# Layer-0 attention on one core: from ten slots to five phases in TensorE's order of work

## What is computed

```python
h, hd = 16, 64
q, k, v = ((x @ w).reshape(4, 1024, h, hd) for w in (w_q, w_k, w_v))
dot = einsum('bqhd,bkhd->bhqk', q / 8, k / 8)
dot = where(causal, dot, -inf)
att = softmax(dot, axis=-1)
out = einsum('bhqk,bkhd->bqhd', att, v).reshape(4, 1024, h * hd) @ w_u + b_u
```

## Time and profile before

| | us |
|---|---|
| median of 3 runs | 2423.7 |
| lowest and highest | 2411.78 and 2423.76 |
| span of the profiled execution | 2408.9 |
| TensorE busy in it | 2199.0 (91%) |
| VectorE busy | 1443.0 (60%) |
| ScalarE busy | 1224.4 (51%) |
| GpSimd busy | 1048.7 (44%) |

### The profile page before, as it was taken

The page is one execution under the profiler, slowest core; times in us unless marked ns, Lnnn a source line. Parts: engine busy times, 40 slices in busy tenths (PEclk is TensorE's granted clock), DMA queues, the critical chain, the costliest instruction groups (busy, mean ns, idle before and its releaser), DMA issues. The chain is left out here.

```text
span 2408.9 us, 40334 instructions
## 1 busy us (share of the span) xinstructions
PE 2199.0 (91%) x15428; PEld 1390.3 (58%) x15428; DVE 1443.0 (60%) x3248; ACT 1224.4 (51%) x1788; POOL 1048.7 (44%) x980
## 2 busy tenths in 40 slices
PE   4999999999999999994999999969999998897787
PEld 2555565555555565543888888724434455555667
DVE  3677757776677757773556565555554555656533
ACT  2555545554465545541323333267786876664533
POOL 0777757776677757773223232433333321100001
PEclk9999999999999999997999999979999999999999
DMA  2000000000000000001200000000000000003001
GB/s 76 1 1 1 1 1 1 1 1 1 1 1 1 1 1 1 1 1 35 39 1 1 1 1 1 1 1 1 1 1 1 1 1 1 2 8 71 1 1 36
DMA packets 36323, 18.19 MB, mean 8 GB/s; under 512 B 16666, under 2 KB 33956, under 8 KB 36132
## 3 DMA queue, kind: packets, MB, share of 16 engines
q1 hardware_dynamic: 36132, 15.61, 2.6%
HBM read 13.50 MB, written 2.10 MB: 6 GB/s over the span
## 5 line engine op out<-in xcount | busy, mean ns | idle before, releaser
L311 POOL TENSOR_TENSOR a_first<-a_first,a_ring 128x512 f32<-128x512 f32 (+3 forms) x352 | 558.8, 1588 | 141.9 <-ACT a_ring L556 106.5
L1764 ACT ACTIVATE g_probsT<-g_s_ps 128x1024 f32<-128x1024 f32 (+2 forms) x448 | 368.9, 868 | 136.6 <-PE g_s_ps L1633 83.3
L556 ACT ACTIVATE a_ring<-a_st 128x768 f32<-128x768 f32 (+1 forms) x256 | 234.6, 916 | 262.8 <-PE a_st L463 262.8
L478 PE MATMUL a_o_ps<-a_ring,a_v 128*64 128x512 f32 (+3 forms) x1280 | 249.2, 485 | 3.4 <-POOL a_ring L293 2.4
L645 DVE RECIPROCAL a_row_inv<-a_row_inv 128x512 f32<-128x512 f32 x64 | 213.8, 3342 | 16.8 <-ACT a_row_inv L544 16.8
L1034 ACT ACTIVATE m_silu<-m_up,m_b 128x512 f32<-128x512 f32 x160 | 109.6, 688 | 221.9 <-PE m_up L966 219.1
L623 DVE TENSOR_REDUCE a_part_max<-a_mx 128x2 f32<-128x1024 f32 x128 | 156.5, 1222 | 102.4 <-PE a_mx L434 99.1
L1664 PE MATMUL g_o_ps<-g_probsT,g_values 128*32 128x512 f32 (+5 forms) x2688 | 206.7, 419 | 5.5 <-POOL g_probsT L1509 5.1
L1633 PE MATMUL g_s_ps<-g_qT,g_kT 64*128 64x512 f32 (+3 forms) x896 | 172.7, 433 | 28.0 <-ACT g_probsT L1764 22.4
L1509 POOL TENSOR_SCALAR_AFFINE_SELECT g_probsT<-g_probsT 128x512 f32<-128x512 f32 x128 | 88.0, 691 | 246.1 <-ACT g_probsT L1764 246.0
L630 DVE CUSTOM_DVE_ANT_0 a_masked<-a_mx,mask_wide,a_part_max 128x256 bf16<-128x256 f32 (+3 forms) x256 | 128.3, 548 | 91.1 <-PE a_mx L434 90.6
(11 more groups left out here) (310 smaller groups left out, 4372.8 us busy)
## 6 DMA issues: line engine op xcount, KB each, us to landing
m_w<-in_L_ffn_rw SPq DMA_DIRECT2D x2, 1024.0 KB, 8.3
s_w<-in_L_ffn_w SPq DMA_DIRECT2D x1, 2048.0 KB, 9.0
s_w<-in_L_ffn_w SPq DMA_DIRECT2D x4, 512.0 KB, 10.2
out_x<-x SPq DMA_DIRECT2D x8, 256.0 KB, 2.3
m_w<-in_L_ffn_rw SPq DMA_DIRECT2D x2, 512.0 KB, 5.1
x<-in_L_attn_x SPq DMA_DIRECT2D x1, 512.0 KB, 4.5
a_outT<-in_L_attn_w_q SPq DMA_DIRECT2D x1, 512.0 KB, 5.4
a_outT<-in_L_attn_w_k SPq DMA_DIRECT2D x1, 512.0 KB, 6.0
```

The lines of the kernel that those rows point to most:

```text
L311: pool.tensor_tensor(total[:, h, q:q + w], total[:, h, q:q + w], probs_of(n, u)[:, h, off:off + w], ALU.add).then_inc(added, 1)
L478: last = pe.matmul(o_ps[rows_of(h), first_q:first_q + w], v_half[n // 4 % 2][:, j, head:head + A_HD], probs_of(n, u)[:, h, off:off + w], s ...
L556: act.activation(probs_of(n, u)[:, :, 0:w], st_ps[u % 2][:, :, 0:w], ACT.Exp).then_inc(exp_done, 1)
L1764: act.activation(out, src.rearrange("p k (j n) -> p k j n", j=at_once), ACT.Exp, scale=float(HD) ** -0.5).then_inc(exp_done, 1)
```

## The change

The ten slots of a pair become five phases t = 0 to 4. In each, TensorE scores units 2t and 2t + 1 and computes the phase's maxima ahead of them, between them and behind them (`MAXES_FIRST`, `MAXES_MIDDLE`, `MAXES_LAST`); then it transposes inputs, does `output` where there is one, weighs units 2t - 2 and 2t - 1 and does `add_rows`; then it does the side work. No instruction of the scores, maxima, values or projections is added or taken away. `output` is split into two column halves of 64, so that it has the form of `weigh`. The value block of phase 1 goes through `mx_ps[:, 0]` instead of `p_ps`. `add_rows(n, 0)` comes in phase 2. The projection k = 0 of a pair moves to the pair before (phase 4) and the order of keys and queries in the second half is exchanged. The loops of ScalarE and VectorE follow the phases; GpSimd's does not change.

```diff
-MAXES_EARLY = {0: (0, 7), 3: (1, 0), 6: (1, 3), 7: (1, 4), 8: (1, 5), 9: (1, 6)}
-MAXES_LATE = {0: (0, 8), 1: (0, 9), 3: (1, 1), 4: (1, 2)}
-PROJECTIONS = {0: 0, 1: 1, 3: 2, 4: 3}
-INVERSES = {2: 0, 5: 1}
-FINISHING = {1: {6: (0, 1), 7: (1, 2), 8: (2, 4), 9: (4, 5)}, 2: {8: (5, 6), 9: (6, 7)}}
-NORMALIZING = {2: {6: (0, 2), 7: (2, 4)}, 3: {2: (4, 5)}}
-BLOCKS_FINISHED, BLOCKS_NORMALIZED = {6: 0, 7: 4}, {6: 0, 8: 4}
+MAXES_FIRST = {0: (0, 7), 2: (1, 1), 3: (1, 3), 4: (1, 5)}
+MAXES_MIDDLE = {0: (0, 8), 1: (1, 0)}
+MAXES_LAST = {0: (0, 9), 2: (1, 2), 3: (1, 4), 4: (1, 6)}
+IS_KEYS = (1, 0, 0, 1)
+PHASES = UNITS_A_PAIR // 2
+PROJECTED_IN = {0: (1, 1), 1: (1, 2), 2: (1, 3), 4: (2, 0)}
+LOW_IN = {0: (1, 0), 1: (1, 1), 2: (1, 2), 3: (1, 3)}
+INVERSES = {1: 0, 2: 1}
+FINISHING = {1: {3: (0, 2), 4: (2, 5)}, 2: {4: (5, 7)}}
+NORMALIZING = {2: {3: (0, 4)}, 3: {1: (4, 5)}}
+BLOCKS_FINISHED, BLOCKS_NORMALIZED = {3: (0, 4)}, {2: (0,), 3: (4,)}
...
+def values_in_maxima(n, t):
+
+    return n >= 0 and t == 1
+
+
+def outputs_of_phase(n, t):
+
+    b, pair = n // PAIRS - 1, n % PAIRS
+    if b < 0:
         return []
-    ahead, k = table[s]
+    if n == ALL_PAIRS:
+        return [(b, k) for k in range(4)] if t == 4 else []
+    return {(0, 4): [(b, 0)], (1, 0): [(b, 1)], (1, 1): [(b, 2)], (1, 2): [(b, 3)]}.get((pair, t), [])
...
+                    if in_maxima:
+                        pe.wait_ge(max_read, m * MAXES + 1)
+                        out = mx_ps[:, 0, :]
+                    else:
+                        take_shared(v_kept, NB * half + blk + 1)
+                        out = p_ps[:]
...
-                            last = pe.matmul(p_ps[:, i * P:(i + 1) * P],
-                                             outT[:, (b * PAIRS + p) % OUT_SLOTS, blk * P:(blk + 1) * P], w_u[:, p, :],
-                                             start=p == 0, stop=p == PAIRS - 1)
+                            rows = outT[:, (b * PAIRS + p) % OUT_SLOTS, blk * P:(blk + 1) * P]
+                            for h in range(2):
+                                last = pe.matmul(p_ps[rows_of(h), i * P:(i + 1) * P], rows[:, rows_of(h)], w_u[:, p, :],
+                                                 start=p == 0, stop=p == PAIRS - 1)
...
-                    pe.wait_ge(max_read, min(MAXES * (n + 2 if c else n + 1) + (0 if c else 3), MAXES * ALL_PAIRS))
+                    pe.wait_ge(max_read, min(MAXES * (n + 2) + 1 if c else MAXES * (n + 1) + 3, MAXES * ALL_PAIRS))
                     pe.wait_ge(added, n * ADDS + ADDS_UP_TO[LAST_OF_CHUNK[c]])
+                    if 2 * n + c:
+                        pe.wait_ge(sums_kept, 2 * n + c)
...
+                    if k == 1:
                         if m > 1:
                             pe.wait_ge(sums_kept, 2 * (m - 1))
+                        for half, blk in values_of_phase(m - 1, 1) if m else ():
+                            pe.wait_ge(v_kept, NB * half + blk + 1)
...
+                def add_up_and_weigh(n, t):
+
+                    if t == 0 and n > 0:
+                        weigh(n - 1, UNITS_A_PAIR - 2)
+                        weigh(n - 1, UNITS_A_PAIR - 1)
+                    if t == 1:
+                        if 0 <= n < ALL_PAIRS:
+                            weigh(n, 0)
+                        if n > 0:
+                            add_rows(n - 1, 1)
+                        if 0 <= n < ALL_PAIRS:
+                            weigh(n, 1)
+                    if t == 2 and 0 <= n < ALL_PAIRS:
+                        weigh(n, 2)
+                        add_rows(n, 0)
+                        weigh(n, 3)
+                    if t > 2 and 0 <= n < ALL_PAIRS:
+                        weigh(n, 2 * t - 2)
+                        weigh(n, 2 * t - 1)
+
...
+                project(0, 0)
                 for n in range(-1, ALL_PAIRS + 1):
                     running, m = 0 <= n < ALL_PAIRS, n + 1
-                    for s in range(UNITS_A_PAIR):
+                    for t in range(PHASES):
+                        for of, k in maxima_of_phase(n, MAXES_FIRST, t):
+                            maxima(of, k)
                         if running:
-                            score(n, s)
-                        for of, k in maxima_of_slot(n, MAXES_EARLY, s):
+                            score(n, 2 * t)
+                        for of, k in maxima_of_phase(n, MAXES_MIDDLE, t):
                             maxima(of, k)
...
+                        if running:
+                            score(n, 2 * t + 1)
+                        for of, k in maxima_of_phase(n, MAXES_LAST, t):
+                            maxima(of, k)
+                        for b, c in inputs_of_phase(n, t):
+                            turn_input(b, c)
+                        for b, part in outputs_of_phase(n, t):
+                            output(b, part)
+                        add_up_and_weigh(n, t)
+                        if t == 2 and m < ALL_PAIRS:
+                            turn_maxima(m, 0)
+                        for half, blk in values_of_phase(n, t):
+                            project_values(half, blk, values_in_maxima(n, t), m)
+                        for of, k in projections_of_phase(n, PROJECTED_IN, t):
+                            project(of, k)
+                        if t == 0 and running:
                             turn_maxima(n, 1)
...
```

More of the change, by code:

```diff
@@ L145, in values_of_slot @@
     half = n // 4 + 1
     if n < 0:
-        groups = {5: (0, 1, 2), 6: (3, 4), 7: (5,), 8: (6,), 9: (7,)}
-        return [(0, blk) for blk in groups.get(s, ())]
-    if half >= HALVES or s not in (2, 5):
+        return [(0, blk) for blk in {1: (0, 1), 2: (2, 3), 3: (4, 5), 4: (6, 7)}.get(t, ())]
+    if half >= HALVES or t not in (1, 3):
         return []
[L151 to L157, removed]
@@ L160, in inputs_of_slot @@
[L160 to L167, removed]
-        return []
-    ahead, k = table[s]
+    return [(half, n % 4 * 2 + t // 3)]
+def values_in_maxima(n, t):
[3 more added lines that the diff above has]
+    if b < 0:
+        return []
+    if n == ALL_PAIRS:
+        return [(b, k) for k in range(4)] if t == 4 else []
+    return {(0, 4): [(b, 0)], (1, 0): [(b, 1)], (1, 1): [(b, 2)], (1, 2): [(b, 3)]}.get((pair, t), [])
@@ L170, in maxima_of_slot, with inputs_of_phase, projections_of_phase, maxima_of_phase @@
+def inputs_of_phase(n, t):
+    return [(n // PAIRS + 1, t - 3)] if n % PAIRS == 3 and n // PAIRS + 1 < BATCH and t >= 3 else []
+def projections_of_phase(n, table, t):
+    if t not in table:
+        return []
+    ahead, k = table[t]
+    return [(n + ahead, k)] if n + ahead < ALL_PAIRS else []
+def maxima_of_phase(n, table, t):
+    if t not in table:
+        return []
+    ahead, k = table[t]
     return [(n + ahead, k)] if 0 <= n + ahead < ALL_PAIRS else []
@@ L385, in project_values @@
                     for i, (a, r) in enumerate(todo):
-                        last = pe.matmul(p_ps[:], a, r, start=i == 0, stop=i == len(todo) - 1)
+                        last = pe.matmul(out, a, r, start=i == 0, stop=i == len(todo) - 1)
                     last.then_inc(v_done, 1)
@@ L503, in _ @@
-                        if m < ALL_PAIRS and s == 5:
-                            turn_maxima(m, 0)
-                        if m < ALL_PAIRS and s in PROJECTIONS:
-                            project(m, PROJECTIONS[s])
-                        for half, blk in values_of_slot(n, s):
-                            project_values(half, blk)
-                        for b, c in inputs_of_slot(n, s):
-                            turn_input(b, c)
-                        for b, t in outputs_of_slot(n, s):
-                            output(b, t)
@@ L522, in keep_projection, with keep_values @@
                     act.activation(out, p_ps[:], ACT.Copy, scale=KEYS_SCALE if qk else 1.0).then_inc(qk_hi_done, 1)
-                def keep_values(half, blk):
+                def keep_values(half, blk, in_maxima):
                     act.wait_ge(v_done, NB * half + blk + 1)
-                    act.activation(v_half[half % 2][:, blk, :], p_ps[:], ACT.Copy).then_inc(v_kept, 1)
+                    src = mx_ps[:, 0, :] if in_maxima else p_ps[:]
+                    act.activation(v_half[half % 2][:, blk, :], src, ACT.Copy).then_inc(v_kept, 1)
                 def keep_input(b, c):
@@ L590, in _ @@
-                        if n % PAIRS == 3 and n // PAIRS + 1 < BATCH and s in BLOCKS_NORMALIZED:
+                            keep_sums(n, 0)
+                        if m < ALL_PAIRS and t == 2:
+                            keep_shift(m, 0)
+                        for half, blk in values_of_phase(n, t):
+                            keep_values(half, blk, values_in_maxima(n, t))
+                        for of, k in projections_of_phase(n, PROJECTED_IN, t):
+                            keep_projection(of, k)
```

102 lines of the change are left out of this document (45 added, 57 removed).

## The result

The changed kernel takes 2432.95 us, the median of 5 runs from 2428.13 to 2433.81; the kernel before, on the same chip, 2417.33, the median of 5 from 2411.78 to 2423.76. The ratio is 1.0058 with a 95% interval of 1.0032 to 1.0083: slower by 0.6%, 15.6 us by the medians. The executions that were profiled have spans of 2408.9 and 2432.0 and differ by 23.1: the one of before was shorter than any of its five timed runs, the one of after among its long ones.

The account below looks back on a forecast made before the run. TensorE's queue was taken to bound the kernel. Ordinary pairs +12 us (+0.39 over 31 pairs), outputs -6 and start +5 made +11 or 12: 2423.7 becomes 2436 us, own range 2412 to 2448, 8 in 10 within 2398 to 2466.

Parts of the forecast that it names:

- The waits that come: TensorE waiting for VectorE's reads of the single maxima tile in ordinary pairs: 1.48 us in phase 0, 0.83 in phase 2.
- 0.25 for the rest: Allowance per pair for waits in phases 1, 3 and 4 and for late values: 0.25 us, ends 0 and 0.8.
- The changes of form: TensorE switching between array shapes, 0.15 or 0.20 us each: from 26 to 15 a pair, giving back 1.9 us.
- the wait of 0.27: A projection standing back for the low part of the one before; expected to go, saving 0.27 us a pair.
- The outputs: Column-split output beside weigh: fewer changes of form and hidden waits, -0.8 - 0.5 - 0.8 a batch, -6 us for three.
- The start: Before the first score, four reads of maxima and an added projection of pair 1: +5 us, ends 0 and 9.
- The layer-norm pieces: Layer-norm work moving with VectorE's and ScalarE's order: taken as 0; one reciprocal later in three batches would be 10 us.
- The end: GpSimd, reciprocals and output at the end of the attention, as before: 0, within 3 us.
- B: Rival: VectorE's reciprocals delay reads that TensorE waits for; 1 us a pair is +31, 2466 us; chance 0.18.
- C: Rival: split output not two at a time, or its weight loads bare; +138 at most, 2574 us; chance 0.02.
- A: Rival: waits hidden, fewer changes of form pay; faster by over 12 us below 1.8 of waits a pair; chance 0.15.
- D: Rival: changes of form and waits cancel, so nothing comes of it; inside the prediction's own range, no separate chance.

## Why the prediction was right, and where it was off

The direction and the size were right: +12 us (0.5%) forecast, +15.6 (0.6%) measured by the medians. That the forecast 2436 lies 3 us from the measured 2432.95 is partly luck: it started from the median of three runs, 2423.7, and that of all five is 2417.33, from which the same sum gives 2429.

Pair by pair the account held. The profiled executions, though, differ by 23.1 us where the sum said 11 to 12. Set against the forecast part by part, the start is 5.2 too small and the third pairs 9.2. The last four intervals and the pairs with inputs gave back 7 that weren't forecast, the end of the attention and the later layers cost 4.5. So the total owes something to misses that cancel. By its steps:

- **TensorE sets the time and a pair is a sum from start to start.** Right. 31.0 a pair forecast, 31.07 to 31.14 measured.
- **The waits that come.** Right one by one: maxima 8 starts 1.71 after maxima 7 (1.70 forecast), maxima 9 1.82 after maxima 8 (1.82), `add_rows` of (n, 0) 1.85 after maxima (m, 2) (1.81). That last wait is missing only in the second pair of a batch, which has an output ahead of it, while the forecast named the first two pairs. The refill of 0.10, taken between 0 and 0.10, is there. The kernels with short reads price them at 1.51, and at 0.85 by difference, where 1.48 and 0.83 stood.
- **0.25 for the rest** (ends 0 and 0.8). Too much. The waits of PE for 400 to 700 us hold nothing of the kind, and 2.35 for all reads is 2.31 and nearly nothing.
- **The changes of form**, -1.9 us a pair. Mis-sized. There are 15 of them, as counted. 11 fewer are worth 1.57 in kernels whose reads are out of the way; the counted -1.9 and the wait of 0.27 that was to go with them together make 2.17, and 31.11 - 30.64 = 0.47 = 2.35 of reads less 1.88. So the gain was 0.3 smaller than the two together, and the 0.25 that I had too much hid most of that. Which of the changes is cheaper than I priced it, wasn't tried; the prediction named this as one of its signs of being wrong.
- **The outputs**, -2.1 a batch. Right: the first two pairs together take 75.54 instead of 76.87, and as two pairs would have cost 0.47 more each, that is -2.3. The split by itself is worth 0.95 of it.
- **The start**, +5 with ends 0 and 9. Mis-sized: +10.2. The waits were +4.2, close to my four reads; what I left out is that TensorE is at a start-to-start of 0.43 there and stayed at it until 66 us. I had priced the work in that stretch with the durations of the earlier trace rows, which are those of the steady state. How long the slow rate lasts isn't the same in every execution: until 47.0, 48.7 and 59.7 us in three kernels with the start of before, until 63.5 to 67.9 in five with the start of after. So +10.2 is a difference of two executions; against the one that was slow until 59.7 it would be 7.
- **The layer-norm pieces**, taken as 0 with an end of 10. The step that failed: +10.4, all in the three third pairs. I had named the end as one reciprocal later in three batches. It is neither a reciprocal nor late data: six tiny VectorE operations that GpSimd's instructions hold up, just ahead of a read that TensorE waits for, and then the half clock. I took them for free, which they nearly are only beside an idle GpSimd. The kernel before already lost 2.3 us at this place in each third pair, and I hadn't looked there.
- **The end**, 0 within 3. The last four intervals gave 3.0 back and the rest of the attention took 2.4. In those intervals the later projections are missing, and the waits of the kernel after are the same three as before; why the loss per pair turns to a gain there wasn't tried.
- **Rivals.** B (in ordinary pairs) and C are refuted by one kernel each. A's point, 1.8 us of waits, fits: measured are 2.35, and with 0.85 of them left (the reads of maxima 7 and 8 short) an ordinary pair takes 29.61, well under 30.64. D was close to the truth for an ordinary pair, 0.47 of 30.64.

## What to carry to other kernels

Grouping work of one form saves little (1.6 us of 30.6 here for 11 changes fewer), and takes from each chain product, read, product the cover that alternation gave it. Before such a regrouping, walk every single-buffered tile: by the rows here the next product can start at start + 0.4 to 0.5 + read + 0.05, and all that TensorE has queued between must cover that. Cost the places that occur a few times (a prologue, a batch's epilogue) by rows of their own stretch: two of them held 20 of the 23 us here. One line of a table won back all of the 5.7 us in each third pair; nine lines of code won back 5 to 12 us at the start, 4.8 of them waits and the rest a clock that differs between executions. And look for a place that is already long in the kernel before: a change of order can lengthen it.

## What the runs showed of the hardware

- A VectorE operation of 128x8 takes 0.16 to 0.17 us beside an idle GpSimd and up to 1.80 beside a working one; the long ones end 0.02 to 0.04 us after GpSimd's instruction.
- A 4.04 us wait of TensorE was followed by a stretch at a granted clock of 0.50 and cost 5.7 us in all, 1.9 of them after the wait. A wait of 2.18 in the kernel before was followed by such a stretch once in three times.
- At the start products follow each other every 0.43 us although the granted clock of that stretch reads 1.00:

```profile
50.00:66.00 16.00, 11.29 (x29) 6.08 (x31) 5.76 (x13) 2.99 (x5) 0.00 (x0) 1.00 0.01 2
```

  The column is no measurement there. The trace's own records of the clock begin at 66.6 us in this execution, with a rise to full, and the view prints 1.00 where there is no record. In the other executions they begin at 48.7 (before), 59.7 (before with split output) and 33.8 (first values in banks of their own), which is where products go from 0.43 to 0.23 apart. Ahead of the first record, the distance of equal products tells the rate. It is that of the 1.2 GHz level: in a stretch that reads 0.50 they are 0.43 apart too.
- 64 instructions of the 64-column form in 3.71 us, with as many weight loads, where 32 of the 128-column form take 3.81: two run at a time, and their loads (3.50 us in all) are hidden though both use all rows.
